# New step numbers and bank turns for a software-pipelined Mamba and FFN kernel

## The reference

```
x = x + 0.5 * ffn(layernorm(x))          # FFN 0
x = x + mamba(layernorm(x))              # with a layernorm and a residual of its own inside
x = x + 0.5 * ffn(layernorm(x))          # FFN 1, same weights
ffn:   xr, xk = mixes of x and the token before it;
       out = sigmoid(xr @ W_r) * (square(relu(xk @ W_k)) @ W_v)
mamba: xs, z = split(layernorm(x) @ W_in)        # 1024 channels each
       xc = silu(conv over 4 tokens of xs)
       dt, B, C = xc @ W_xproj                   # 32 + 16 + 16
       delta = softplus(dt @ W_dt + b_dt)
       h[t] = exp(delta*A) * h[t-1] + delta*B*xc      # 16 states for each channel
       y = sum over states of h*C + D_skip*xc
       out = (y * silu(z)) @ W_out
```

## Time and profile before

| | us |
|---|---|
| median of the three runs | 4891.49 |
| lowest and highest | 4890.23, 4892.57 |
| span of the profiled execution, first to last instruction | 4888.0 |
| VectorE busy | 4488.3 (92%) |
| TensorE busy | 4296.9 (88%) |
| GpSimd busy | 3196.4 (65%) |
| ScalarE busy | 2900.1 (59%) |
| granted TensorE clock, mean | 0.971 |

### The profile page before, as it was taken

The page is one execution under the profiler, slowest core; times in us unless marked ns, Lnnn a source line. Parts: engine busy times, 40 slices in busy tenths (PEclk is TensorE's granted clock), DMA queues, the critical chain, the costliest instruction groups (busy, mean ns, idle before and its releaser), DMA issues.

```text
span 4888.0 us, 58099 instructions
## 1 busy us (share of the span) xinstructions
PE 4296.9 (88%) x16896; PEld 2382.9 (49%) x16896; DVE 4488.3 (92%) x3650; ACT 2900.1 (59%) x6355; POOL 3196.4 (65%) x3328
## 2 busy tenths in 40 slices
PE   6777989898999989989898899989999898999787
PEld 2444545454554545545454454545545454554443
DVE  2799999999999999999999999999999999999992
ACT  2555656666666566656666665666656666665452
POOL 1666767576676767767576676767667576776770
PEclk9888999999999999999999999999999999999798
DMA  2445555454554555555555554555555565655451
GB/s 82 141 135 180 172 171 185 163 183 162 189 169 151 189 168 186 172 173 185 158 174 163 186 172 152 190 179 176 172 185 173 155 180 156 190 170 153 167 164 62
DMA packets 423053, 810.71 MB, mean 166 GB/s; under 512 B 41264, under 2 KB 41264, under 8 KB 418640
## 3 DMA queue, kind: packets, MB, share of 16 engines
q1 hardware_dynamic: 422736, 807.00, 52.1%
HBM read 772.25 MB, written 34.60 MB: 165 GB/s over the span
## 4 chain that ended last, share of the span: by engine, by line
DVE 38%; PE 29%; issue 16%; ACT 7%; POOL 6%; DMA 3%; DVEq 0%; SPq 0%; POOLq 0%; ACTq 0%
DVE decay L1091 19%; DVE g L1099 10%; PE y_acc L567 6%; PE mm L494 5%; PE mm L483 5%; POOL dbx L1298 4%; PE mm L472 4%; DVE xc L1037 3%; DMA c_all<-bc_scratch 2%; PE mm L531 2%; PE mm L509 2%; PE mm L519 2%; DVE xc L1043 1%; ACT decay L889 1%; POOL xout L1287 1%
## 5 line engine op out<-in xcount | busy, mean ns | idle before, releaser
L1298 POOL TENSOR_TENSOR dbx<-u,b_all 128x1024 f32<-128x1024 f32 x1024 | 2414.2, 2358 | 902.6 <-DVE g L1099 901.7
L1091 DVE TENSOR_TENSOR_SCAN decay<-decay,state,dbx 128x1024 f32<-128x1024 f32 x1024 | 2405.4, 2349 | 172.4 <-ACT decay L889 157.6
L567 PE MATMUL y_acc<-ident,g 128*128 128x128 f32 x8192 | 1124.2, 283 | 372.5 <-DVE g L1099 370.6
L567 PEld LDWEIGHTS y_acc<-ident,g 128*128 128x128 f32 x8192 | 947.4, 144 | 939.1 <-DVE g L1099 713.2
L1099 DVE TENSOR_TENSOR g<-decay,c_all 128x1024 f32<-128x1024 f32 x1024 | 1244.3, 1215 | 10.0 <-DMA c_all<-bc_scratch 1.1
L886 ACT ACTIVATE decay<-delta,neg_a 128x512 f32<-128x512 f32 x1024 | 708.7, 692 | 36.9
L889 ACT ACTIVATE decay<-delta,neg_a 128x511 f32<-128x511 f32 x1024 | 686.9, 671 | 0.0
L895 ACT ACTIVATE state<-decay 128x2 f32<-128x2 f32 x1024 | 166.9, 163 | 508.6 <-DVE g L1099 506.1
L494 PE MATMUL mm<-wbuf_c,col 128*128 128x512 f32 x1024 | 460.9, 594 | 2.1 <-ACT col L758 1.3
L1037 DVE SCALAR_TENSOR_TENSOR xc<-mm,conv_sb,xc 128x509 f32<-128x509 f32 (+2 forms) x384 | 285.3, 743 | 47.0 <-ACT xs_last L804 35.7
L1302 POOL TENSOR_TENSOR dbx<-dbx,carry 128x1 f32<-128x1 f32 x1024 | 274.2, 268 | 80.3
(11 more groups left out here) (100 smaller groups left out, 5107.4 us busy)
## 6 DMA issues: line engine op xcount, KB each, us to landing
b_all<-bc_scratch SPq DMA_DIRECT2D x1024, 256.0 KB, 3.4
c_all<-bc_scratch SPq DMA_DIRECT2D x1024, 256.0 KB, 3.6
wbuf_d<-in_w_r SPq DMA_DIRECT2D x32, 1024.0 KB, 7.5
wbuf_c<-in_w_v SPq DMA_DIRECT2D x32, 1024.0 KB, 7.3
xin<-in_x SPq DMA_DIRECT2D x16, 1024.0 KB, 6.8
wbuf_c<-in_w_k SPq DMA_DIRECT2D x16, 1024.0 KB, 6.7
wbuf_d<-in_w_in SPq DMA_DIRECT2D x16, 1024.0 KB, 5.8
wbuf_a<-in_w_in SPq DMA_DIRECT2D x16, 1024.0 KB, 8.0
```

The source lines that it names most:

```text
L567: last = pe.matmul(y_acc[:, tb, j * P:(j + 1) * P], g[:, s % PAIRS, j, tb * P:(tb + 1) * P], ident[:, :], start=n == 0 and j == 0 and tb % ...
L1091: dve.tensor_tensor_scan(d, d, flat(dbx[:, s % DBX, :, :]), state[:, batch, s, 0:1], ALU.mult, ALU.add).then_inc(scan_done, 1)
L1298: pool.tensor_tensor(dbx[:, s % DBX, :, :], u[:, q % 2, :, :], b_all[:, s % BRING, :].unsqueeze(1).broadcast_to([P, QT, W]), ALU.mult).the ...
```

## The change

Only numbers in the tables change. A piece of work keeps its instructions and gets another step, and products get another of the two banks. ZEROS alone changes a count: eight zero matmuls a chunk become two. SP's loads and stores move as well.

```diff
-        TURN = ((0, 0, 1, 1), (35, 35, 35, 35))
-        YTURN = (31, 31, 39, 39, 61, 61, 66, 66)
+        TURN = ((0, 0, 1, 1), (34, 34, 35, 35))
+        YTURN = (31, 31, 39, 40, 60, 60, 65, 66)
         DT = (-11, 3, 18, 33)
-        SUM_SKIP = (5, 27, 35, 53)
+        SUM_SKIP = (6, 26, 35, 52)
         OUT = ((4, 5), (19, 20), (21, 22), (23, 23))
-        MM_K = ((5, 7, 8, 9), (46, 47, 50, 51))
-        MM_R = ((10, 10, 12, 13), (41, 42, 44, 45))
-        MM_V = ((14, 15, 16, 17), (54, 55, 56, 57))
+        MM_K = ((5, 7, 7, 9), (47, 48, 51, 51))
+        MM_R = ((10, 10, 12, 12), (41, 42, 43, 45))
+        MM_V = ((14, 15, 16, 16), (54, 54, 55, 57))
         MTURN = (25, 25, 26, 26)
-        Z = (27, 29, 32, 37, 58, 59, 60, 62)
-        XS = (28, 30, 34, 36, 38, 40, 43, 46)
+        Z = (27, 29, 32, 37, 58, 59, 59, 62)
+        XS = (28, 29, 34, 36, 38, 40, 43, 46)
         XPROJ = (49, 50)
-        ZEROS = {2: 2, 31: 2, 39: 2, 30: 1, 53: 1}
-        KEEP_Y = (17, 33, 49, 65)
-        COLUMNS = ((1, 1, 2, 2), (36, 36, 36, 36))
-        BEFORE_K = ((3, 3, 5, 5), (39, 39, 40, 40))
-        BEFORE_R = ((6, 7, 7, 7), (37, 37, 38, 38))
-        RELU = ((7, 8, 9, 10), (49, 50, 53, 53))
-        TANH = ((11, 13, 14, 14), (42, 43, 45, 46))
+        ZEROS = {31: 1, 25: 1}
+        KEEP_Y = (17, 33, 49, 64)
+        COLUMNS = ((1, 1, 2, 2), (35, 36, 36, 37))
+        BEFORE_K = ((2, 2, 5, 6), (40, 40, 40, 43))
+        BEFORE_R = ((3, 6, 6, 6), (40, 40, 40, 40))
+        RELU = ((7, 8, 9, 10), (50, 50, 52, 53))
+        TANH = ((11, 13, 13, 14), (43, 43, 45, 46))
         DELTA = (-10, 4, 19, 34)
-        SKIP = (-6, 14, 31, 43)
-        INNER = (24, 24, 24, 24)
-        MCOLS = (26, 26, 27, 27)
-        RES = (25, 25, 25, 25)
-        NORM = ((58, 58, 58, 58), (31, 31, 31, 31))
-        GATE_TANH = (28, 31, 33, 38, 59, 60, 61, 63)
-        TAP0 = (29, 31, 35, 37, 39, 41, 44, 47)
-        CTANH = (30, 32, 37, 38, 40, 42, 45, 48)
+        SKIP = (-9, 14, 29, 41)
+        INNER = (23, 24, 24, 25)
+        MCOLS = (26, 27, 27, 27)
+        RES = (23, 25, 25, 26)
+        NORM = ((58, 59, 59, 59), (31, 31, 31, 31))
+        GATE_TANH = (29, 31, 33, 39, 60, 60, 61, 63)
+        TAP0 = (29, 31, 35, 37, 40, 41, 44, 48)
+        CTANH = (32, 35, 39, 39, 41, 46, 46, 48)
         XROWS = 51
-        MIX_K = ((3, 4, 5, 5), (42, 43, 45, 46))
-        MIX_R = ((6, 7, 7, 8), (38, 39, 40, 40))
-        CSILU = (33, 34, 40, 42, 43, 45, 48, 48)
+        MIX_K = ((3, 4, 5, 5), (42, 43, 46, 46))
+        MIX_R = ((5, 7, 7, 9), (40, 40, 40, 40))
+        CSILU = (34, 40, 42, 42, 42, 49, 49, 49)
         GATE_SILU = (28, 30, 33, 38, 59, 60, 61, 63)
-        GATE_Y = (31, 32, 39, 40, 61, 62, 66, 66)
+        GATE_Y = (31, 32, 39, 41, 61, 63, 66, 67)
         GATE = ((15, 16, 18, 18), (55, 56, 57, 58))
-        OUT_ADD = (6, 22, 23, 25)
-        STATS = ((51, 53, 53, 54), (9, 22, 24, 27), (18, 19, 20, 21))
+        OUT_ADD = (6, 21, 23, 25)
+        STATS = ((48, 52, 52, 52), (9, 22, 24, 27), (18, 18, 19, 21))
         MEANS = (56, 27, 21)
         TAPS = (29, 31, 35, 37, 39, 41, 44, 47)
-        MAKE_U = (-8, 9, 27, 38)
-        FFN_ADD = ((18, 19, 20, 22), (57, 58, 59, 60))
+        MAKE_U = (-8, 10, 31, 41)
+        FFN_ADD = ((19, 19, 21, 23), (58, 58, 60, 61))
         RSTD = (58, 30, 24)
         HISTORY = 26
-        ADD_HEAD = (32, 34, 38, 40, 42, 44, 47, 50)
-        LOAD = {"wo1": 0, "res": 2, "wv0": 11, "wxs0": 15, "wz0": 19, "wk1": 25, "wxs1": 26, "res_out": 26, "wr1":
-                38, "wv1": 39, "x": 47, "wr0": 47, "wo0": 48, "bc_out": 52, "wz1": 53, "wk0": 59, "out": 61}
-        BANK = {"f0T": (1, 0, 1, 0), "YT": (0, 0, 1, 1, 1, 1, 1, 0), "dt": (0, 1, 1, 0, 1, 0, 0, 1), "o": (0, 1, 0,
-                1), "f0k": (1, 0, 1, 0), "f0r": (1, 0, 1, 1), "f0v": (1, 0, 1, 0), "mT": (1, 0, 1, 0), "z": (0, 0,
-                1, 1, 0, 1, 0, 0), "xs": (1, 1, 0, 0, 0, 0, 0, 0), "f1T": (1, 1, 0, 1), "f1r": (1, 1, 1, 1), "f1k":
-                (1, 0, 0, 1), "xp": (1,), "f1v": (0, 1, 0, 1)}
+        ADD_HEAD = (32, 35, 39, 40, 42, 46, 47, 50)
+        LOAD = {"wo1": 3, "res": 2, "wv0": 13, "wxs0": 23, "wz0": 20, "wk1": 25, "wxs1": 29, "res_out": 29,
+            "wr1": 40, "wv1": 39, "x": 47, "wr0": 50, "wo0": 48, "bc_out": 50, "wz1": 54, "wk0": 61, "out":
+            60}
+        BANK = {"f0T": (0, 1, 0, 0), "YT": (0, 0, 1, 1, 1, 1, 1, 0), "dt": (0, 1, 1, 0, 1, 0, 0, 1), "o":
+            (0, 1, 0, 1), "f0k": (1, 0, 1, 1), "f0r": (1, 0, 0, 1), "f0v": (1, 0, 1, 0), "mT": (0, 1, 0, 0),
+            "z": (0, 0, 1, 1, 0, 1, 0, 0), "xs": (1, 1, 0, 0, 0, 0, 0, 0), "f1T": (1, 1, 1, 1), "f1r": (1,
+            1, 1, 1), "f1k": (1, 0, 0, 1), "xp": (1,), "f1v": (0, 1, 0, 1)}
```

## The result

The changed kernel takes 4923.5 us (median of 4 runs, 4920.9 to 4927.1) against 4892.0 for the kernel before on the same chip. The ratio is 1.0065, with an interval from 1.0051 to 1.0079: slower by two thirds of a per cent, where 4880 was forecast, and outside the range of 4850 to 4912.

The account below looks back on a forecast made before the run. VectorE, busy 4488.3 of 4888.0 us, was taken as the bound, with only its idle time to win. Stretch terms summed to -0.7 us a chunk, -11 over 16 chunks, from the 4891.5 median to 4880; range 4850 to 4912.

Parts of the forecast that it names:

- The loads at the boundary: Loads that move otherwise (wv0, wo1, wr1, wz1, wk0) still go out at least one landing ahead of use.
- The 0.3 us for keep_y 3: Steps 0 to 9: keep_y 3, ahead of decay 1, awaits the old chunk's last sum; scan 1 some 0.3 us late.
- the landing time L: Steps 20 to 31: time the rows1 store takes to land, holding up step 31's norm; taken as 9.0 us.
- Steps 0 to 9: Chunk's start: waits at scan 1 and f0T3 against a gain in step 7's mixes; sum +0.2 us a chunk.
- rival (4): TensorE's clock dips with fewer zero matmuls, reaching the full queue of steps 4 to 9: 4908 us, chance 0.09.
- The mixes: Step 7: with u1 one POOL step later, the long mix loses about 0.6 us; POOL waits for a running mix.
- u1 holds the second mix: Step 7: by the skill's shared-port rule u1 blocks a mix for a whole POOL product; no gain instead of -11 us.
- Steps 10 to 19: Step 15's 3.62 us wait becomes about 1.4 and 1.1; TensorE's work holds the stretch's end; -0.3 us a chunk.
- Steps 20 to 31: Gains of 1.6 us offset by the later rows1 store, which step 31's norm waits for; 0.0 a chunk.
- Rival (1): Steps 20 to 31: the store lands no sooner than before, 10.0 to 11.1 us; 4896 to 4913 us, chance 0.20.
- Steps 49 to 58: Step 52's 4.05 us wait goes, waits of 2.4 and about 1.5 come, 1.5 of work comes in; +0.4 a chunk.
- The third sign: Whole chunk: the forecast is wrong if the granted clock is at half for more than 5 us a chunk.

Follow-up runs that it names:

- d_loads: c_front with only the change's loads put in again (wk0 61, out 60, wo1 3, wv0 13, wxs0 23): 4889.7 us.
- d_turns: c_front with z6, YT4 to YT6, the gate tanh, gate_y and keep_y 3 as changed: 4895.3 us.
- g_clk2: d_turns with two zero matmuls added at step 62: 4889.4 us.
- d_ffn0: c_front with the FFN 0 lists of steps 1 to 17 as changed, u1 left at POOL's step 9: 4884.6 us.
- f_rv: c_front with r3 at step 12, v3 at 16, tanh 2 at 13 and r3's bank as changed: 4873.0 us.
- c_front: The changed kernel with the store at step 26 and all entries in steps 59 to 19 as before: 4870.9 us.
- a_zeros: The changed kernel with ZEROS as before, eight zero matmuls a chunk: 4922.2 us.
- e_wxs1: The changed kernel with only the load wxs1 back from step 29 to 26, the store staying at 29: 4893.7 us.
- b_store: The kernel before with the store res_out at step 29 for 26, wxs1 left at 26: 4892.3 us.
- a_store: The changed kernel with the store res_out back from step 29 to 26: 4895.5 us.
- g_best: c_front with FFN 1's residual adds on POOL a step earlier and two more norms at step 58: 4857.1 us.

## Why the prediction was wrong, point by point

In short: three terms of the sum failed. The loads at the boundary, put at nothing, made the multiply of step 0 wait for c_all (d_loads: 1.0 us a chunk). The 0.3 us for keep_y 3 is its price at full clock only (d_turns: 0.72 in the mean). And the landing time L was taken as 9.0 us and measured 9.8.

**What bounds the kernel: right.** VectorE's work fell, its idle time grew, and the whole difference is idle time.

**Steps 0 to 9, +0.2 forecast, +1.1 measured: the largest miss.** Two terms failed. First, "keep_y 3 moves ahead of decay 1 ... scan 1 some 0.3 us late": the mechanism was right and the price was that of full clock. g_clk2 shows 0.34 at full clock; with the sum at half clock it is up to 1.22, and 0.72 in the mean of d_turns. In after itself most of it is hidden behind the second one. I had rival (4), the half clock, at "the full queue of steps 4 to 9"; it struck at step 0, in a sum of eight small matmuls that had just become critical. Second, "the loads that move otherwise still go out at least one landing ahead of use". I had looked only at whether the moved loads themselves land in time. They do. But out and wk0 go out 2.6 us apart and later than before, wk0 1.0 us ahead of the c_all load of step 0, and that load lands in 10.0 us for 8.4 and goes out 1.0 us later. d_loads shows what this costs alone: 1.0 us at step 0. The term for f0T3, decay 3 "about 0.5 late", did not show before scan 3 in after; waits before scans 5 and 9 did (0.28 and 0.36 in the mean), which were not foreseen.

**The mixes: the gain came, the reading behind it was wrong.** Step 7 gained what was forecast (4.89 us for 5.49). But the prediction took from the earlier trace rows that POOL waits for a running mix, and not the mix for POOL. Those rows do not show that, and the traces show that it goes both ways: whoever comes second waits. In each of the twenty traces, the mixes and silus that start while POOL still works on dbx or u, all with their inputs in SBUF, end 0.55 us behind the end of that product (median), and take from 0.67 up to 2.1 us by what is left of it (2.45 in d_ffn0); the gates and output additions of the same size, which read one operand from PSUM, take 0.66 to 0.69 us beside it. Step 7 in after and in d_ffn0 (chunk 7):

```profile
2234.61 2.38 POOL L1299 TENSOR_TENSOR dbx<-u,b_all 128x1024 f32<-128x1024 f32 x1 [1.36 <-DVE g L1100]
2236.61 1.60 DVE L1020 SCALAR_TENSOR_TENSOR xn_col<-col,vec,xn_col 128x512 f32<-128x512 f32 x2
...
2237.55 2.87 POOL L1277 TENSOR_TENSOR u<-delta,xc 128x1024 f32<-128x1024 f32 x1
```

```profile
2224.39 2.36 POOL L1297 TENSOR_TENSOR dbx<-u,b_all 128x1024 f32<-128x1024 f32 x1
...
2225.29 2.67 DVE L1018 SCALAR_TENSOR_TENSOR xn_col<-col,vec,xn_col 128x512 f32<-128x512 f32 x2
```

In after, dbx ends at 2236.99, 0.4 us after the mixes begin, and they take 1.60; u, which starts between the two, takes 2.87 instead of its 2.37. So the case that the prediction weighs, that u1 holds the second mix, did not come true, since the mix was first and u was the one to wait. In d_ffn0, as in before, u stands ahead of this dbx, which therefore ends later (2226.75), and the mixes take 2.67. What the move of u1 won is time in which mixes stood still beside POOL.

**Steps 10 to 19: right.** Both waits to 0.1 us, the stretch to 0.13, and by f_rv the claim that TensorE's work holds its end. Scan 20 came at 87.7 after the chunk's start, all of the delay brought along from steps 0 to 9. (The forecast says 86.5; from before's 86.7 and the sum of -0.1 it should say 86.6.)

**Steps 20 to 31, 0.0 forecast, +0.5 measured.** The mechanism, the moment of issue (127.6 for 126.9) and the gain without the store (52.22) were right. The failed step is "I take 9.0, nearer to the median than to the least"; it was 9.8. Worse than the size was the reason: I took the landing time for a matter of traffic. The trace of before had the same pair, wxs1 just ahead of the store, behind its median of 10.0, and after keeps that pair together; the landing stayed what it was. Rival (1), at 0.20, was the one that came true here, though its total, at most 4913, did not hold. The wait is worth 2.15 us a chunk, 28 us of the program.

**Steps 32 to 48: -1.05 for -1.1**, right in the sum and partly by luck. VectorE's work fell by 1.9 us for the 1.5 of the forecast, and its idle time grew by 0.9 for 0.4 (0.62 and 0.22 of it stand before convolution taps in steps 37 and 47, behind ScalarE's xs_last, which was not among the terms).

**Steps 49 to 58, +0.4 forecast, +0.9 measured.** The waits were named rightly: 2.71 for 2.4 before scan 55, 1.15 for 1.5 before scan 59, and 1.6 us of work came in for 1.5. A wait of 0.34 before scan 52 was missed, and the 0.3 at scan 55 is the sizing of TensorE's 18.1 us. No step was wrong in kind.

**Steps 59 to 63, +0.1 forecast, +0.5 measured.** I counted only VectorE's work. Moving z6, YT4 and YT5 up by a step puts YT5, and z7 behind it, into a wait for gate_y 4, and the silu of step 63 into one for z7.

**The ends.** Behind the last scan 5.2 us were lost that the sum did not hold at all. In the trace, one gate multiplication more on VectorE ahead of the last multiply, the out products (30.2 us for 29.3) and the first r product of FFN 1, at 60.6 for 56.6 us after the last scan's start, can be seen; none of it was tried, so the cause stays open. Some 2 us of such a difference can be chance: c_front and f_rv, which do not differ there, have 110.9 and 112.6. Ahead of the first scan nothing changed (153.6 in both). The prediction's 158.2 is the start of the second scan, not of the first; its sum does not use the difference.

**The sum.** -0.7 a chunk forecast, +1.8 measured: 1.1 of the 2.5 us between them from steps 0 to 19, 0.5 each from 20 to 31, 49 to 58 and (0.4) 59 to 63. All misses have one sign. The stretches were priced as if each began with everything in its place, and what is missing from the sum is the boundary, where three engines and the DMA queue come together.

**The signs.** Scan 20 stayed inside its bounds (87.7, between 85 and 88) and norm waited for the store, 3.3 us. The third sign, half clock for more than 5 us a chunk, was met: the mean granted clock over chunks 2 to 13 is 0.992 in before and 0.977 in after, which makes some 4.6 and 13.4 us a chunk at half clock. It was a poor sign all the same: c_front has 0.983, some 9.7 us a chunk, and is 22 us faster than before.

**On the clock.** The Trainium skill (TensorE: Matmul & The Clock Gate, section HAM oscillation — how this bites in real kernels) has idle gaps between bursts bring the half clock back. g_clk2 agrees: 1.7 us of fillers in such a gap took the sum from 1.86 to 1.09 us. a_zeros shows the other side: it has six zero matmuls a chunk more than after, none of them ahead of that sum, which still took more than 1.4 us at 9 of 15 boundaries, and the time did not change.

## What to carry to other kernels

Where a cyclic schedule is moved, price the boundary first, and for every large transfer ask not only whether it lands in time but what small, just-in-time loads are issued behind it; a store that is waited for should have no other large transfer still under way ahead of it on its queue. Compare a landing time with the one at the same place of the other trace, not with the median of the run. A single undo that gives nothing does not clear its suspect: where several waits of different engines lie side by side, take them all away together, then put each one back. And moving one entry of a table moves its partners' deadlines: the head add left at step 46 cost 150 us.

## What the runs showed of the hardware

A store of 1 MB lands in 5.5 us (e_wxs1) and 5.7 us (b_store) when no other megabyte has gone out for 12 us; in 9.8 us when one goes out 0.5 us ahead (after); and in 9.5 us (a_store) and 8.8 us (g_best) when one goes out 2.6 us ahead.

Loads of 256 KB that land in 3.7 us in the median of the run take 8.4 to 8.9 (after, 2489 to 2502) near a store and a load of 1 MB each. The one that step 0 needs takes 8.4 us where the two were issued 5.7 and 0.5 us ahead of it (before) and 10.0 us where they were issued 3.6 and 1.0 us ahead (after). In the same stretch the issue itself grows on SP: 1.52 us for a load whose issue otherwise takes 0.32; before shows up to 1.39 at its own boundary.

A mix or silu of VectorE (512 columns, inputs in SBUF) that starts during a POOL product over 1024 columns ends 0.55 us after that product in the median of every trace: two mixes took 1.60 us with 0.4 us of the product left (after) and 2.67 with 1.5 us left (d_ffn0). Gates and output additions of the same size, with one input in PSUM, take 0.66 to 0.69 us beside it.

Eight small matmuls take 1.09 us at full clock and 1.97 us at half clock (d_turns).
